# Perceiver layer in fp32: one fp32 unit and eight of rounded halves per pair of heads, and re-ordered last steps, maxima and column halves

## Time and profile before

| | |
|---|---|
| time, median of 3 | 609.17 us (608.8 to 609.3) |
| the profiled execution | 609.33 us, its span 607.6 us, mean granted TensorE clock 1.000 |
| TensorE products busy | 598.5 us (99%) |
| TensorE weight loads busy | 527.5 us (87%) |
| VectorE | 463.8 us (76%) |
| ScalarE | 376.5 us (62%) |
| GpSimd | 202.5 us (33%), nearly all of it in the attention |
| DMA | 120.66 MB, mean 199 GB/s |

### The profile page before, as it was taken

The page is one execution under the profiler, slowest core; times in us unless marked ns, Lnnn a source line. Parts: engine busy times, 40 slices in busy tenths (PEclk is TensorE's granted clock), DMA queues, the critical chain, the costliest instruction groups (busy, mean ns, idle before and its releaser), DMA issues.

```text
span 607.6 us, 10751 instructions
## 1 busy us (share of the span) xinstructions
PE 598.5 (99%) x3924; PEld 527.5 (87%) x3924; DVE 463.8 (76%) x911; ACT 376.5 (62%) x655; POOL 202.5 (33%) x164
## 2 busy tenths in 40 slices
PE   9999999999999999999999899999999999999997
PEld 8888888899899899999998789999989999997573
DVE  5613138678888888888887868979999998989783
ACT  5123125668687867787776535699688787787110
POOL 0000002287878787779784811220010000000000
DMA  7501011877788778887878937657867757798400
GB/s 298 204 0 36 1 43 37 214 203 213 209 216 210 206 185 209 209 218 199 217 181 223 343 146 204 242 203 282 314 221 290 275 221 285 276 370 338 183 1 17
DMA packets 29969, 120.66 MB, mean 199 GB/s; under 512 B 7729, under 2 KB 8113, under 8 KB 22497
## 3 DMA queue, kind: packets, MB, share of 16 engines
q1 hardware_dynamic: 29488, 119.22, 62.0%
q10 hardware_dynamic: 432, 0.79, 0.3%
HBM read 86.30 MB, written 0.26 MB: 142 GB/s over the span
## 4 chain that ended last, share of the span: by engine, by line
PE 84%; DVE 9%; ACT 3%; issue 3%; DVEq 0%; POOL 0%; ACTq 0%
PE ps L1906 18%; PE ps L1596 13%; PE ps L1597 13%; PE ps L1598 13%; PE ps L1641 4%; PE ps L1703 4%; PE ps L1781 3%; PE ps L1966 3%; PE ps L1946 2%; PE ps L2078 2%; PE ps L1665 2%; PE ps L2041 2%; DVE prob_far L1199 2%; DVE pt_lo L1082 1%; DVE prob_far L1223 1%
## 5 line engine op out<-in xcount | busy, mean ns | idle before, releaser
L1906 PEld LDWEIGHTS ps<-norm_t,ring 128*128 128x128 f32 x1152 | 131.7, 192 | 2.9 <-issue 1.7
L1906 PE MATMUL ps<-norm_t,ring 128*128 128x128 f32 x1152 | 133.4, 276 | 0.0
L592 POOL TENSOR_TENSOR pt_lo<-far_t,pt_hi 128x512 fp32r<-128x512 f32 (+1 forms) x94 | 112.0, 1215 | 57.7 <-ACT pt_hi L697 57.6
L768 ACT ACTIVATE prob_far<-prob_far,neg_max 128x1024 f32<-128x1024 f32 (+2 forms) x96 | 85.5, 892 | 41.0 <-DVE neg_max L1203 41.0
L1199 DVE TENSOR_SCALAR_CACHE_REDUCE prob_far<-ps 128x256 f32<-128x256 f32 (+2 forms) x96 | 86.7, 906 | 31.1 <-PE ps L1598 30.7
L1223 DVE STREAM_TRANSPOSE prob_far<-prob_far 128x2176 f32<-128x2176 f32 x30 | 73.1, 2436 | 0.8 <-ACT prob_far L768 0.2
L1390 DVE SCALAR_TENSOR_TENSOR acc<-raw,cw,acc 128x127 f32<-128x127 f32 (+2 forms) x240 | 65.8, 349 | 3.7 <-ACT acc L946 3.1
L1596 PE MATMUL ps<-pt_hi,v_hi 128*128 128x256 f32 x208 | 60.7, 292 | 2.1 <-DVE pt_lo L1082 1.5
L1596 PE MATMUL ps<-k_hi,q_hi 128*128 128x512 f32 (+2 forms) x160 | 61.2, 383 | 1.0 <-DVE prob_far L1199 0.3
L697 ACT ACTIVATE pt_hi<-far_t 128x512 fp32r<-128x512 f32 (+1 forms) x105 | 57.8, 589 | 2.4 <-DMA far_t<-prob_far 1.8
L1598 PE MATMUL ps<-pt_lo,v_hi 128*128 128x256 f32 x208 | 58.8, 282 | 0.0
(11 more groups left out here) (246 smaller groups left out, 1233.2 us busy)
## 6 DMA issues: line engine op xcount, KB each, us to landing
ring<-w_in_dram SPq DMA_DIRECT2D x36, 1024.0 KB, 5.0
far_t<-prob_far SPq DMA_DIRECT2D x240, 136.0 KB, 2.9
ring<-w_out_dram SPq DMA_DIRECT2D x16, 1024.0 KB, 5.4
ring<-wq_dram SPq DMA_DIRECT2D x16, 512.0 KB, 4.6
ring<-wo_dram SPq DMA_DIRECT2D x16, 512.0 KB, 3.4
w_sb<-w_dram SPq DMA_DIRECT2D x4, 896.0 KB, 10.5
ring<-w_dram SPq DMA_DIRECT2D x3, 1024.0 KB, 9.2
ring<-ctx_t_dram SPq DMA_DIRECT2D x2, 1024.0 KB, 5.5
```

The source lines that it names most:

```text
L592: sub = lambda dst, a, hi: pool.tensor_tensor(dst, a, hi, ALU.subtract)
L768: nc.scalar.activation(tile, tile, ACT.Exp, bias=neg_max[:, b, h:h + 1], accum_out=part_sum[:, b, h, i:i + 1]).then_inc(exp_ok, 1)
L1906: ins = mm(ps[:, bank, t * T:t * T + T], w[:, t, c, :], norm_t[:, c, :], start=(c == 0), stop=(c == NC - 1))
```

## The change

Units: `FP32_TILES` keeps unit 0 alone (tiles 15, 16); units 1 to 7 are two tiles of halves each (0 to 13), unit 8 the tile 14. The value halves have 15 tiles, of which two lie in tensors of their own (`V_HOME`, `high_of`, `low_of`), with a fourth part to split. ScalarE's `first_fars` are units 1 and 2, then 3 and 4; each later place takes the unit before the one it had (5 for 6, 6 for 7, 7 for 8), and unit 8 comes behind the first exponential of head 1. GpSimd splits units 1 to 5 first, at p = 2 then the wo low half, and 6, 7 and 8 with the key chunks behind them; VectorE keeps unit 5 at p = 0 and has none at p = 1.

VectorE's order in a step: the third piece of head 0 is read ahead of `o_split` and the second addition, and `invert` is divided into `sum_rows` and the reciprocal.

Steps 13 to 15: GpSimd does wo's low half in step 13 behind unit 5, and in step 14 waits for VectorE's subtractions (low_ok) before it does the last two.

Tail: the last tile group of the product back to 512 columns goes as two halves of 256 columns into banks 2 and 3, and VectorE adds and does the statistics (`bn_stats`) half by half; the last part of w1's low half goes to GpSimd; nine warm-up products for twelve; the last product of the feed-forward is in halves of 256 columns (banks 4 and 5), and so are the last addition and the transfer of the result.

```diff
...
-FP32_TILES = {0: (13, 14), 1: (15, 16)}
+FP32_TILES = {0: (15, 16)}
 FAR0 = len(FP32_TILES)
-V_TILES = 13
-V_PARTS = ((0, 2), (2, 8), (8, 13))
+V_TILES = 15
+V_HOME = 13
+V_PARTS = ((0, 2), (2, 8), (8, 13), (13, 15))
...
-LOW_U = {0: 5, 1: 7}
+LOW_U = {0: 5}
...
-    return 9 * n + u - 3 if u >= FAR0 + SLOTS else 9 * n + u - 5
+    return 9 * n + u - 3 if u >= FAR0 + SLOTS else 9 * n + u - 4
...
+                far_split(n, 1)
+                if p == 0 and kv:
+                    v_split(kv, 1)
                 for u in (2, 3, 4):
                     far_split(n, u)
                 if p == 0 and kv:
                     v_split(kv, 2)
                 else:
                     far_split(n, 5)
-                if p == 2:
-                    wo_split(n - 1)
+                if p == 0:
+                    v_split(kv, 3)
+                if p == 2 or n == LAST_PAIR - 2:
+                    wo_split(n - (p == 2))
                 if p == 3:
                     v_split(kv + 1, 0)
                 far_split(n, 6)
                 if keys:
                     k_split(kv + 1, 0)
-                    k_split(kv + 1, 1)
-                if p != 1:
-                    far_split(n, 7)
-                if keys:
-                    k_split(kv + 1, 2)
+                far_split(n, 7)
                 far_split(n, 8)
                 if keys:
-                    k_split(kv + 1, 3)
-                    k_split(kv + 1, 4)
+                    for i in range(1, NCHUNK):
+                        k_split(kv + 1, i)
                 if p != 1:
                     wo_split(n)
-                if p == 3:
-                    v_split(kv + 1, 1)
-            for u in range(2, 5):
+            for u in range(1, 5):
                 far_split(LAST_PAIR - 1, u)
-            wo_split(LAST_PAIR - 2)
+            pool.wait_ge(low_ok, dve_lows(LAST_PAIR - 1, 8))
...
+            pool.wait_ge(ug_ok, 2 * GROUPS)
+            pool.wait_ge(w1h_ok, NC)
+            sub(w1_lo[:, NC - 1, :], w1_sb[:, NC - 1, :], w1_hi[:, NC - 1, :].bitcast(F32)).then_inc(w1l_ok, 1)
...
+                far(n, p, 1)
                 far(n, p, 2)
-                far(n, p, 3)
...
+                far(n, p, 3)
                 far(n, p, 4)
-                far(n, p, 5)
                 wo_split(n, 2 * kv + p // 2, p % 2)
                 if p == 0 and not begin:
                     v_split(kv, 2)
+                    v_split(kv, 3)
                 if p == 3:
                     act.wait_ge(pv_ps, 9 * n + 3)
                     v_split(kv + 1, 0)
                 soft_exp(n + 2, b, 0, 1)
                 if ask:
-                    far(n, p, 6)
+                    far(n, p, 5)
                 if keys:
                     act.wait_ge(s_ps, 6 * n + 16)
                     k_split(kv + 1, 0)
                 soft_exp(n + 2, b, 0, 2)
                 soft_exp(n + 2, b, 0, 0)
-                far(n, p, 7 if ask else 6)
+                far(n, p, 6 if ask else 5)
                 if keys:
                     act.wait_ge(s_ps, 6 * n + 17)
                     k_split(kv + 1, 1)
-                far(n, p, 8 if ask else 7)
+                far(n, p, 7 if ask else 6)
                 if keys:
                     k_split(kv + 1, 2)
                 soft_exp(n + 2, b, 1, 1)
+                far(n, p, 8 if ask else 7)
...
+                far(n, 2, 3)
                 far(n, 2, 4)
+                wo_split(n, 2 * kv + 1, 0)
                 far(n, 2, 5)
-                wo_split(n, 2 * kv + 1, 0)
                 far(n, 2, 6)
                 last_plain(0)
                 far(n, 2, 7)
-                last_plain(1)
                 far(n, 2, 8)
+                last_far(1)
                 last_far(2)
...
+            def sum_rows(m, b):
                 dve.wait_ge(exp_ok, 2 * NPC * (m + 1))
                 nc.vector.tensor_reduce(row_sum[:, b, :], part_sum[:, b, :, :], AX_X, ALU.add).then_inc(sum_ok, 1)
+
+            def invert(m, b):
                 dve.wait_ge(sum_ok, m + 1)
+                if not (isinstance(m, int) and m < 2):
+                    dve.wait_ge(wo_ev, 2 * (m - 1))
                 nc.vector.reciprocal(row_inv[:, b, :], row_sum[:, b, :]).then_inc(inv_ok, 1)
...
                 scores_out(n + 2, b, 0, 1, sent)
+                sum_rows(n, b)
+                scores_out(n + 2, b, 0, 2, sent)
                 if not (isinstance(n, int) and n < 1):
                     o_split(n - 1, 1 - b)
                 if not (isinstance(n, int) and n < 2):
                     add_pair(n - 2, b, 0)
+                scores_out(n + 2, b, 1, 0, sent)
                 invert(n, b)
-                scores_out(n + 2, b, 0, 2, sent)
-                scores_out(n + 2, b, 1, 0, sent)
                 if p == 0 and not (isinstance(n, int) and n == 0):
                     far_split(n, p, LOW_U[0])
                 scores_out(n + 2, b, 1, 1, sent)
                 scores_out(n + 2, b, 1, 2, sent)
-                if p == 1:
-                    far_split(n, p, LOW_U[1])
...
-            w1_split(3)
             dve.wait_ge(var_s, 6)
-            slot, before = out_chunk(GROUPS - 1, 1)
+            slot, before = out_chunk(GROUPS - 1, 0)
             dve.wait_ge(freed[slot], before + 1)
             nc.vector.scalar_tensor_tensor(res[:], ps[:, 6, :], rstd[:, 2:3], res[:], ALU.mult,
                                            ALU.add).then_inc(res_ok, 1)
             dve.wait_ge(res_ok, 1)
+            dve.wait_ge(left_cols, 1)
+            nc.vector.scalar_tensor_tensor(res[:, 0:2 * P], ps[:, 2, 0:2 * P], rstd[:, 2:3], res[:, 0:2 * P],
+                                           ALU.mult, ALU.add).then_inc(res_ok, 1)
+            dve.wait_ge(res_ok, 2)
+            nc.vector.bn_stats(stats[:, 0, :], res[:, 0:2 * P]).then_inc(left_stats, 1)
+            slot, before = out_chunk(GROUPS - 1, 1)
+            dve.wait_ge(freed[slot], before + 1)
+            nc.vector.scalar_tensor_tensor(res[:, 2 * P:], ps[:, 3, 0:2 * P], rstd[:, 2:3], res[:, 2 * P:],
+                                           ALU.mult, ALU.add).then_inc(res_ok, 1)
+            dve.wait_ge(res_ok, 3)
...
+            for h in range(2):
+                cols = slice(2 * P * h, 2 * P * h + 2 * P)
+                dve.wait_ge(ffn_ps, h + 1)
+                nc.vector.tensor_tensor(final[:, cols], res[:, cols], ps[:, 4 + h, 0:2 * P],
+                                        ALU.add).then_inc(final_ok, 1)
...
-                elif u in (4, 5):
-                    pe.wait_ge(last_hi, u - 3)
-                elif u > 5:
-                    pe.wait_ge(last_lo, u - 5)
+                elif u == 4:
+                    pe.wait_ge(last_hi, 1)
+                elif u > 4:
+                    pe.wait_ge(last_lo, u - 4)
...
+            def last_out_proj():
+
+                slot, before = out_chunk(GROUPS - 1, 1)
+                w = ring[slot][:].rearrange("p (t n) -> p t n", t=4)
+                pe.wait_ge(landed[slot], (before + 1) * 16)
+                for h in range(2):
+                    for t in range(4):
+                        ins = mm(ps[:, 2 + h, 0:2 * P], ug[1][:, 4 + t, :], w[:, t, 2 * P * h:2 * P * h + 2 * P],
+                                 start=(t == 0), stop=(t == 3))
+                    ins.then_inc(freed[slot] if h else left_cols, 1)
+
+            pe.wait_ge(ug_ok, 2 * GROUPS)
+            last_out_proj()
+
+
+            for _ in range(LAST_WARM):
...
+                tiles_ = range(4 * i, min(4 * i + 4, NFT))
+                pieces = [(t, h) for t in tiles_ for h in range(2)] if i < 3 else [(t, h) for h in range(2) for t in tiles_]
+                for t, h in pieces:
+                    at = (t % 4) * DM + 2 * P * h
+                    ins = mm(ps[:, 4 + h, 0:2 * P], hsel_t[:, t, :], ring[s][:, at:at + 2 * P],
                              start=(t == 0), stop=(t == NFT - 1))
-            ins.then_inc(ffn_ps, 1)
+                    if t == NFT - 1:
+                        ins.then_inc(ffn_ps, 1)
...
```

More of the change, by code:

```diff
@@ L88 @@
 WARM = 12
+LAST_WARM = 9
 RING = 6
@@ L122, in pool_lows @@
 def pool_lows(n, u):
-    skipped = (n + 2) // 4 + max(0, (n - 1) // 4) + any(by_dve(n, v) for v in range(u))
+    skipped = max(0, (n - 1) // PAIRS) + any(by_dve(n, v) for v in range(u))
     return FAR_UNITS * n + u - FAR0 + 1 - skipped
 def dve_lows(n, u):
-    if n < LAST_PAIR - 1:
-        return n // 2 + n % 2
-    return 7 + u - 4
+    return n // PAIRS if n < LAST_PAIR - 1 else KVH - 1 + u - 4
 def build(nc, x, ctx_q, ctx_t, wq, wk, wv, wo, w_in, w_dt, w_out, conv_w, conv_b, dt_bias, a_log, d_skip,
@@ L577, in _ @@
                 load(s, w2[c] if c < 3 else w2_tail[0], before)
-            sp.wait_ge(final_ok, 1)
-            sp.dma_start(out, final[:]).then_inc(stored, 16)
-            sp.wait_ge(stored, 16)
+            for h in range(2):
+                cols = slice(2 * P * h, 2 * P * h + 2 * P)
+                sp.wait_ge(final_ok, h + 1)
```

(38 more changed lines are left out.)

38 lines of the change are left out of this document (25 added, 13 removed).

## The result

The changed kernel takes 630.54 us (median of 4 runs, 628.23 to 632.86) against 609.21 for the kernel before on the same chip: 1.035 times as long (95% interval 1.031 to 1.039). The forecast was 627.0. The profiled execution is the longest of the four, 632.86 (span 631.1).

What follows compares the result with a forecast made beforehand. TensorE's own work was taken to bound the kernel, each new wait adding to the end. On 609.33 us: 21.2 + 1.6 + 3.8 - 2.4 - 5.5 - 1.0 = +17.7, giving 627.0 us; range 615 to 634.

Steps and rivals of the forecast that it cites:

- p = 3: Attention steps of this kind: TensorE waits for unit 6, 1.05 us per step.
- p = 0: Attention steps of this kind: only the wait for unit 6, 1.05 us; the fourth value part was costed at nothing.
- p = 1: Attention steps of this kind: a copy of keys on ScalarE precedes unit 6, so the wait is 1.36 us.
- p = 2: Attention steps with wo ahead of unit 6 on GpSimd: 2.73 us there, 0.86 at the next step's unit 1, 3.59 total.
- step 0: First attention step: 1.05 us at unit 6, about 0.5 for an extra early ScalarE copy, 1.6 total.
- step 13: Attention step asking for no next pair: waits of 0.74 us for unit 5 and 3.05 for unit 6, 3.8 total.
- Unit 6: Chain from the fifth scores chunk's end to unit 6 ready: 6.61 us against 5.67 needed; 1.05 late with the restart.
- rival A: GpSimd's queue does no harm in the attention: only 1.05 us per step, 617 us; chance 0.14.
- rival C: Four waits of 3 us and more cost TensorE its clock, 2.3 us each: 636 us; chance 0.07.
- What goes away: TensorE's earlier waits in the attention and last pairs, 5.7 us, go except 0.3, with restarts: -5.5 us.
- The halves: One fp32 unit per pair becomes halves on TensorE: 0.15 us saved, times 16 pairs, -2.4 us.
- Rival B: No new wait at unit 6 in the attention, so faster: 600.4 us; chance 0.09.

Runs made afterwards that it cites:

- run of the small parts: Kernel before with the tail's column halves, the last pairs' order and VectorE's earlier maxima, but two fp32 units and seven of halves as before: 605.12 us.
- filler run: Changed kernel with nine dummy TensorE products in the idle time ahead of unit 6 in steps 2, 6, 10 and 13: 627.95 us.
- the two orders: Changed kernel with ScalarE rounding unit 6 right behind unit 5, and GpSimd making wo's low half ahead of unit 5 (p = 2, step 13): 620.09 us.
- first edit: Changed kernel with ScalarE copying unit 6 right behind unit 5, ahead of two exponentials: 628.38 us.

## Why the prediction was right, and where not

The chain that the prediction followed, from the scores through VectorE, ScalarE and GpSimd to unit 6, is what the rows show, and it carries the result. That the sum agrees to 0.1 us with the profiled execution less the clock (626.9) is in part luck: several terms were off by 0.4 to 2.3 us and largely cancel.

What a step lost in the changed kernel is its length less that of the run of the small parts (15.50, 15.58 at p = 1), plus the 0.15 that one fp32 unit less saves. The steps with p = 2 and step 13 are taken from the filler run, so without half clock.

| term | forecast | measured |
|---|---|---|
| p = 3 | 1.05 | 1.01 |
| p = 0 | 1.05 | 1.22 |
| p = 1 | 1.36 | 1.23 |
| p = 2 | 3.59 | 3.57 |
| three rounds of four | 21.2 | 21.1 |
| step 0 | 1.6 | 1.25 |
| step 13 | 3.8 | 2.93 |
| clock in steps 2, 6, 10, 13 | 0 | 1.4 to 1.6 each, when it falls |

The first point reads these rows of TensorE in step 3:

```profile
173.48 0.34 PE L1639 MATMUL ps<-k_lo,q_hi 128*128 128x384 f32 x1
...
179.37 0.28 PE L1639 MATMUL ps<-pt_lo,v_hi 128*128 128x256 f32 x1
180.40 0.39 PE L1637 MATMUL ps<-pt_hi,v_hi 128*128 128x256 f32 x1 [0.74 <-POOL pt_lo L605]
```

- **Unit 6.** Right in place and size. The fifth chunk ends at 173.82. TensorE could start unit 6 at 179.49, 5.67 later, and gets it at 6.58 (forecast 6.61, or 6.57 by the spacing of 1.26 on GpSimd); the first product then holds it 0.10 longer. The row says [0.74] for this, not 0.91, as idle is counted from the modelled end of a product of 0.28, where the next could start after 0.12. The bracket alone misses about 0.27 of the 1.01 that such a wait costs.
- **p = 0.** The sum came by another way than I gave: 0.33 of idle at unit 2, behind value part 1, and 0.19 at unit 6. The wait at unit 2 comes after the fifth chunk, so it uses up most of the time by which unit 6 is late. I had costed the value parts at nothing. The run that moves ScalarE's copy of part 1 behind unit 1 took 2.06 us off a kernel whose steps with p = 0 had such a wait, so that copy is the cause there; in the changed kernel the idle at unit 2 has the same place and size (0.33).
- **p = 2.** Unit 6 came 2.55 late with the restart (forecast 2.73), unit 1 about 1.0 (0.86). Both GpSimd's place for wo and the backlog out of p = 1 were real: the first is worth 5.6 us with step 13, and 8.1 with the clock; the second stayed when the two orders were mended. So rival A fell.
- **Step 13** was 0.9 too dear: unit 5 came 0.45 and unit 6 2.57 idle, and the same step had 0.33 of waits before which went.
- **Clock.** I gave this to rival C at 0.07 only. Its mechanism is real, at 1.4 to 1.6 us a place and not 2.3, and in some executions only. It took idle times of 2.29 to 2.57, not the waits "of 3 us and more" that the rival spoke of (my own sum had 2.62 at p = 2). It was no part of my sum; with the sum's 627.0 against 626.9 (profiled execution less the clock) and 627.95 (filler), it is what the median of 630.54 has beyond the forecast.
- **What goes away.** Forecast -5.5 and -1.0 for the tail; measured -4.2 for all of it, and 0.43 more in step 14 of the changed kernel, where step 13's waits give units 1 to 4 their time. I had let all of the waits of the earlier trace rows but 0.3 go, yet the run of the small parts keeps 2.3 (GpSimd's pt_lo 1.2, the score reads 0.8, q_lo 0.3). Step 13's 0.9, step 0's 0.35 and this 0.43 cancel most of it, and that is the luck in the sum.
- **The halves.** Right: steps with no wait take 15.35 to 15.37 at p = 3 and p = 0 for 15.48 to 15.50. But the run with value part 1 behind unit 1 gains only 1.3 us over the small parts in its other steps, since those with p = 2 gain 0.03 each (15.47 for 15.51). And it loses 1.85 in step 14 (11.32 for 9.97), step 0 (14.84 for 14.49) and step 8 (15.65 for 15.51). In steps 14 and 0 TensorE now idles 1.07 and 0.26 for pt_lo ahead of its early units of halves; I take it that the second fp32 unit, which needs no preparation, covered this before. So even with the orders mended the exchange comes out even: 605.51 against 605.12.

Rival B (no new wait) fell with 22 waits. What made the change slow is not the number of subtractions as such but their place: kernels with the same eight units of halves took 630.5, 620.1 and 605.5 us, by order alone down to 620.1, and by order and engine together from there.

## What to carry to other kernels

Before work is moved from a full engine to three half idle ones, follow one item through all queues, from the event that releases it to the instruction that needs it, and compare with the time that the item has; here that sum gave the loss of each step from 1 to 12 to 0.2 us, while the busy shares said that there was room. Queue long work that is ready early ahead of a short piece that comes late and is waited for. A wait on TensorE has two prices, its own length and, behind the waits of 2.3 to 2.6 us here, a possible stretch at half clock; a few products without use inside the wait took most of the second away. And when runs scatter by clock, take such a stretch off the executions that have it and not off the median.

## What the runs showed of the hardware

**Half clock after a short idle.** Waits of TensorE of 2.29, 2.32 and 2.57 us were followed by products at 1.2 GHz in the execution shown; the one of 2.32 in step 6 was followed by nine products at full clock, and the slow ones came 1.5 us after the restart:

```profile
232.57 0.39 PE L1637 MATMUL ps<-pt_hi,v_hi 128*128 128x256 f32 x1 [2.32 <-POOL pt_lo L605]
...
233.86 0.41 PE L1639 MATMUL ps<-ring_lo,o_hi 128*128 128x512 f32 x1
234.10 3.58 PE L1744 MATMUL ps<-norm_t,ring 128*128 128x128 f32 x16
237.34 0.45 PE L1637 MATMUL ps<-pt_hi,v_hi 128*128 128x256 f32 x1
```

The same sixteen products took 2.19 in step 2, partly at full clock. In the first edit's profiled execution a wait of 2.32 in the same place had no slow product behind it. A shorter idle can perhaps do it too. The kernel before is at a mean clock of 0.997 in 11 of 56 executions, some 2 us longer (611.1 for 609.1), and so are the tail alone in 4 of 12 and the maxima alone in 4 of 11; all three have step 14's wait of 1.53. In none of the 35 executions of kernels in which that step's order is mended and no wait is over 2 us did the clock fall that far. So the fall goes with step 14's order. That the wait of 1.53 is what brings it is inferred: no profiled execution caught it, and among the 35 are five with three waits of 1.61 each, in other steps, and no fall, so length alone doesn't settle it. The Trainium skill (TensorE: Matmul & The Clock Gate, What's actually happening) has two levels, and a gate that recent activity sets, not in step with the kernel; the rows agree: two levels, and the same wait costs it or not.

**VectorE beside GpSimd.** A subtraction of 128x512 with both inputs in SBUF took 0.69 when GpSimd was idle and 1.28 beside GpSimd's pt_lo (the rows of the last pairs' order alone). Of the three in the earlier trace rows the first, beside GpSimd's pt_lo for most of its time, took 1.24, and the two beside its wo subtractions 2.88 and 2.58; GpSimd's own took 2.8 instead of 2.4 there. The Trainium skill (SBUF — State Buffer, Who interferes with whom) says that a VectorE instruction with two SBUF inputs contends with a GpSimd instruction that reads SBUF: the trace agrees, in both directions. The last pairs' order alone, which keeps the two apart, was worth 2.0 us.
